# First layer of a graph network: a round's gathers in four groups, each issued at its own place of the round

## The chip, the cores and the metric

One core of a Trainium2 chip runs the whole program. The metric is the device time of one execution in microseconds (us). The core's engines are named as in the profile: PE (TensorE, matmuls; PEld its weight loads), DVE (VectorE), ACT (ScalarE), POOL (GpSimd), SP (SyncE, which here issues plain transfers). All transfers run on the core's 16 DMA engines.

## What is computed

3125 nodes with 256 features, 50000 edges sorted by their target node. Two layers, each followed by a residual and a layer norm:

```python
k, q, v = (typed_linear(x, W, ntype) for W in (Wk, Wq, Wv))       # (n, 8, 32)
# per edge e: source src[e], target dst[e], type r = etype[e] of 5
a  = ((k[src] @ Ratt[r]) * q[dst]).sum(-1) * pri[r] / sqrt(32)
w  = softmax of a over the edges that share a target
h  = segment_sum((v[src] @ Rmsg[r]) * w, dst)
h  = typed_linear(h, Wa, ntype)
x1 = layernorm(x + h * alpha + x * (1 - alpha))                   # alpha = sigmoid(skip)[ntype]

msg = (x1 @ weight[rel])[src] * norm * sigmoid(x1 @ gate_weight[rel])[src]   # 16 relations
out = layernorm(x1 + relu(segment_sum(msg, dst)))
```

## The kernel before

The nodes are cut into 26 tiles of 121 (ROUNDS = 26), and the edges of one tile, at most 2048 of them, are laid out as 128 partitions x 16 columns (U = 16, in G = 4 groups of GU = 4 columns). Three stages follow one another:

1. Tables. For each node and each of 5 edge types k·Ratt and v·Rmsg go to a table in HBM (`kv_table`, 2 KB a row), the queries to another.
2. First layer, 26 rounds, one per tile. For each of 16 columns POOL issues one indirect DMA (a gather): 128 rows of 2 KB, 256 KB in all, picked from `kv_table` into `kv[:, par, u]`, where par is the round's parity (two buffers). A line of 16 row numbers tells which rows. DVE multiplies with the queries that PE hands out (`score`, L1369 to L1376), takes a softmax along and across partitions, weighs the values (`weigh`, L1462), and PE sums them by target node (`aggregate`, L863) into the PSUM tile `b_agg`. The tile of the round before is finished meanwhile: `normalise` (L1382 to L1394, DVE) divides by the softmax sum, `turn_h` (L803) and `project` (L811, PE) apply Wa into `b_out`, `stats` (L1401, DVE) adds the residual, `norm_rows` gives x1. The tile two rounds back has its 16 relation products made: `message` (L835, PE, 8 chunks), `keep_message` (L1097, ACT) and `store_messages` (L495, SP, 4 stores of 484 KB into `message_table`).
3. Second layer, 26 turns: gathers from `message_table`, a sum by target, a norm.

Each engine works its own instructions off in the order in which the code gives them, and semaphores tie the engines together. PE's order in a round r (function `l0` of the PE block; f is the round before, n the next): turn_h(f, 0), message 0, hand_queries(r, 3), turn_h(f, 1), turn_ends(r) (L842), message 1, project(f), turn_carry(r) (L848), messages 2 and 3, turn_back(r) (L854), one-hot turns and queries of n, messages 4 and 5 between them, aggregate(r, 0 to 3) with queries of n between, messages 6 and 7. DVE's order: score(r, 0), score(r, 1), normalise(f), row_index(n), score(r, 2), score(r, 3), softmax scans, stats(f), make_onehot(n), softmax_across, norm_rows(f), softmax_less, weigh.

POOL's gathers are in `gather(pair)`: for each parity it waits for `idx_ready[par]` and then issues all 16 gathers of that round one behind another. `idx_ready` comes from DVE's `row_index` (L1358), which copies the 16 row numbers of the next round from `rows` into a small tile `idx`. That copy stands behind `normalise(f)`, which waits for `agg_done`, one count a round, given by the last aggregate matmul; it is therefore also what tells POOL that the buffer of round r + 1 (last used by round r - 1 = f) is free:

```python
dve.wait_ge(agg_done, f.done)          # in normalise(f), then behind it:
v.tensor_copy(idx[:, r.par, :], rows[:, 0, ...]).then_inc(idx_ready[r.par], 1)
```

The DMAs that SP issues in a round are: queries of the next round (242 KB), its x (121 KB), four message stores (4 x 484 KB), one x1 store (121 KB).

## Time and profile before

| | |
|---|---|
| median of 3 runs | 2108.01 us (2104.2 to 2119.34) |
| the profiled execution | 2111.33 us, its span 2109.7 us |
| PE busy | 1386.6 us, 66% |
| DVE busy | 926.7 us, 44% |
| POOL busy | 854.6 us, 41% |
| tables, until about | 340 us |
| first layer, about | 340 to 1462 us |
| second layer, about | 1462 to 2109.7 us |

The profile of one execution has a page (busy time of the engines, forty slices of the span, groups of instructions with their idle time and what ended it) and a trace that can be asked for the instructions of a stretch in order of time. Behind an instruction stands, in brackets, how long its engine sat idle before it and what ended that: a line of the kernel, "issue" (nothing that the profile shows), or "remote" (a semaphore moved, but no recorded instruction ended just then). PE's instructions are recorded when they start; their ends are modelled.

### The profile page before, as it was taken

The page shows a single profiled execution, that of the slowest core. Times are in us where ns is not written, and L with a number is a line of the kernel's source. Part 1 is how long each engine was busy: PE and PEld are TensorE (multiplying, and loading weights), DVE is VectorE, ACT ScalarE, POOL GpSimd, SP SyncE. Part 2 cuts the span into 40 slices and gives each one's busy share as a digit, 9 for nine tenths or more (in the row PEclk, how much of TensorE's full clock was granted, in tenths as well). Part 3 has the DMA queues.
Part 4 walks back from the last instruction along what each step waited for, and adds up shares of the span by engine and source line. Part 5 has one row for each costly group of instructions (what it writes and reads, how often), then busy time and mean ns, then how long its engine had stood idle before and what let it go on. Part 6 is the DMA issues. An engine that isn't in the chain of part 4 may idle for free.

```text
span 2109.7 us, 21535 instructions
## 1 busy us (share of the span) xinstructions
PE 1386.6 (66%) x6758; PEld 1135.8 (54%) x6758; DVE 926.7 (44%) x1940; ACT 494.7 (23%) x1069; POOL 854.6 (41%) x905
## 2 busy tenths in 40 slices
PE   4899985785797667777677776679425444445444
PEld 3888884574675556665466655567313322233323
DVE  5533454764564455454465544654212322223321
ACT  2223322232333333233243332335100000000000
POOL 1130004754244332233432334320575666666662
PEclk8999996798798878889888887789656666656666
DMA  5444465655445544445544455443433333333331
GB/s 122 124 147 144 135 227 157 183 181 174 136 142 176 161 146 137 133 134 160 178 145 142 149 157 176 141 136 95 115 109 89 104 104 104 104 94 107 108 104 53
DMA packets 103847, 286.54 MB, mean 136 GB/s; under 512 B 20804, under 2 KB 40408, under 8 KB 100660
## 3 DMA queue, kind: packets, MB, share of 16 engines
q0 software_dynamic: 56032, 169.34, 26.6%
q1 hardware_dynamic: 47774, 116.71, 18.3%
q8 instruction: 19, 0.31, 0.1%
q14 instruction: 22, 0.18, 0.0%
HBM read 189.33 MB, written 96.65 MB: 136 GB/s over the span
## 4 chain that ended last, share of the span: by engine, by line
PE 46%; issue 23%; another core or an unknown queue 12%; DVE 8%; DMA 5%; ACT 2%; POOL 2%; SPq 1%; DVEq 0%; ACTq 0%; POOLq 0%
PE bank L953 12%; PE bank L863 9%; PE bank L835 8%; PE bank L727 4%; PE bank L793 4%; DMA kv_table<-tstage 4%; PE bank L781 3%; DVE kv L1371 2%; PE bank L749 1%; POOL kv L649 1%; PE bank L735 1%; DVE onehot_r L1363 1%; PE bank L755 1%; DVE S L1376 1%
## 5 line engine op out<-in xcount | busy, mean ns | idle before, releaser
L633 POOL DMA_INDIRECT kv<-kv_table,idx x416 | 424.1, 1019 | 637.9 <-DVE idx L1358 514.7
L649 POOL DMA_INDIRECT kv<-message_table,rows x416 | 394.4, 948 | 274.1 <-issue 123.4
L953 PE MATMUL bank<-kv,onehot_w 128*121 128x256 f32 x832 | 274.7, 463 | 338.0 <-issue 307.2
L953 PEld LDWEIGHTS bank<-kv,onehot_w 128*121 128x121 f32 x832 | 186.2, 226 | 426.5 <-issue 391.0
L835 PE MATMUL bank<-wr_r,x1T_r 128*121 128x512 f32 x1248 | 359.5, 433 | 34.9 <-issue 22.7
L835 PEld LDWEIGHTS bank<-wr_r,x1T_r 128*121 128x121 f32 x1248 | 235.7, 200 | 95.2 <-issue 28.5
L1097 ACT ACTIVATE mstage<-bank,gate 121x256 f32<-121x256 f32 x416 | 171.4, 471 | 245.3 <-PE bank L835 132.7
L863 PE MATMUL bank<-kv,onehot_r 128*121 128x264 f32 x832 | 204.0, 394 | 0.0
L1512 DVE SCALAR_TENSOR_TENSOR z<-bank,xb 121x256 f32<-121x256 f32 x26 | 10.9, 420 | 425.5 <-remote 280.8
L863 PEld LDWEIGHTS bank<-kv,onehot_r 128*121 128x121 f32 x832 | 151.3, 187 | 29.5
L854 PE MATMUL bank<-ident,carry 8*128 8x8 f32 x26 | 6.2, 237 | 241.9 <-DVE carry L1441 220.3
L1371 DVE TENSOR_TENSOR kv<-kv,bank 128x512 f32<-128x512 f32 x208 | 132.1, 674 | 42.9 <-issue 33.4
L1175 ACT ACTIVATE sd<-mv,eps 121x1 f32<-121x1 f32 x26 | 7.7, 295 | 604.5 <-DVE mv L1518 506.2
L793 PE MATMUL bank<-qb_r,onehotT_r 121*128 121x256 f32 x832 | 139.5, 316 | 10.5 <-DVE kv L1371 10.5
L854 PEld LDWEIGHTS bank<-ident,carry 8*128 8x128 f32 x26 | 4.5, 172 | 253.7 <-issue 253.7
L1401 DVE TENSOR_TENSOR z<-z,bank 121x256 f32<-121x256 f32 x26 | 11.0, 421 | 293.4 <-remote 261.3
L793 PEld LDWEIGHTS bank<-qb_r,onehotT_r 121*128 121x128 f32 x832 | 125.1, 216 | 15.5 <-issue 11.5
L1376 DVE TENSOR_REDUCE S<-kv 128x32 f32<-128x1024 f32 x104 | 127.1, 1222 | 10.7
L1532 DVE TENSOR_SCALAR onehot_w<-iota_n,dstl,norms 128x121 f32<-128x121 f32 x416 | 111.9, 361 | 33.0 <-issue 21.6
L1462 DVE TENSOR_TENSOR kv<-kv 128x1024 f32<-128x1024 f32 x104 | 120.4, 1220 | 13.5 <-ACT kv L1107 12.0
L727 PE MATMUL bank<-xmT_r,w_r 128*128 128x484 f32 (+1 forms) x504 | 112.2, 386 | 12.7 <-DVE tstage L1298 10.6
L1055 ACT ACTIVATE onehotT_r<-bank 121x512 fp32r<-121x512 f32 x104 | 62.2, 598 | 222.9 <-PE bank L781 221.3
(136 smaller groups left out, 1647.1 us busy)
## 6 DMA issues: line engine op xcount, KB each, us to landing
message_table<-mstage SPq DMA_DIRECT2D x104, 484.0 KB
kv_table<-tstage SPq DMA_DIRECT2D x26, 1210.0 KB
kv<-kv_table,idx POOLq DMA_INDIRECT x416
kv<-message_table,rows POOLq DMA_INDIRECT x416
query_table<-qstage_r SPq DMA_DIRECT2D x26, 242.0 KB
qb_r<-query_table SPq DMA_DIRECT2D x26, 242.0 KB
kv<-in_Wr POOLq DMA_DIRECT2D x2, 2048.0 KB, 14.8
xb<-in_x SPq DMA_DIRECT2D x26, 121.0 KB
```

The source lines that it names most:

```text
L633: pool.indirect_dma_start(kv[:, par, u, 0:2 * C], None, ktab, bass.IndirectOffsetOnAxis(ap=idx[:, par, u:u + 1], axis=0)).then_inc(kv_land ...
L649: pool.indirect_dma_start(mrows[:, r.q, u, :], None, mtab, bass.IndirectOffsetOnAxis(ap=rows[:, 1, r.number, u:u + 1], axis=0)).then_inc(l ...
L727: last = mm(b[:, 0:plan.width], lhsT, rhs, start=(n == 0), stop=(n == len(terms) - 1))
L793: last = mm(b_qe[pr % 2][:, q * C:(q + 1) * C], onehotT_r[:, 2 * pr + q, :], qb_r[:, r.par, part, :], start=(part == 0), stop=(part == 1))
L835: last = mm(b_m[c % 2][:NODES, :], x1T_r[:, f.par, a, h, :], wr_r[:, w, h, 2 * c:2 * c + 2, :], start=(n == 0), stop=(n == len(terms) - 1))
L863: last = mm(b_agg[:NODES, 0:C + H], onehot_r[:, r.par, u, :].bitcast(F32), kv[:, r.par, u, C:ROW], start=(u == 0), stop=(u == U - 1))
L953: last = mm(b_l[r.q][:NODES, 0:C], onehot_w[:, r.q, u, :], mrows[:, r.q, u, :], start=(u == 0), stop=(u == U - 1))
L1097: last = a(mstage[:, b % 2, q % (RT // PARTS), :], b_m[c % 2][:NODES, k * C:(k + 1) * C], ACT.Copy, scale=gate[:NODES, f.par, q:q + 1])
L1371: ins = v.tensor_tensor(k, k, b_qe[pr % 2][:, :].rearrange("p (a c) -> p a c", a=2), ALU.mult)
L1376: v.tensor_reduce(S[:, :, u:u + 4].rearrange("p h u -> p u h"), kv[:, r.par, u:u + 4, 0:C].rearrange("p u (h d) -> p u h d", h=H), AX.X, A ...
L1462: v.tensor_tensor(w, w, e, ALU.mult).then_inc(weighted[g], 1)
L1532: last = v.tensor_scalar(onehot_w[:, r.q, u, :], iota_n[:, :], dstl[:, j, u], norms[:, j, u], ALU.is_equal, ALU.mult)
```

## The change

A round's 16 gathers are issued as four groups of four, and each group waits at its own place of the round. With n the round that is gathered for, into the buffer last used by round n - 2:

- group 0 waits until aggregate group 0 of round n - 2 is done,
- group 1 until all of round n - 2 is aggregated,
- group 2 also until `ends_turned` has counted n, so until turn_ends of round n - 1 (L842 of before) is done on PE,
- group 3 until `carryT` has counted n, so until turn_carry of round n - 1 (L848 of before) is done on PE.

For this `agg_done` counts each group of aggregate matmuls (4 a round). The gathers read their row numbers in `rows` itself, so `row_index`, its tile's use here and `idx_ready` go. POOL's loop over pairs of rounds is written out as 26 rounds.

```diff
-            def gather(pair):
-
-                for par in range(2):
-                    settle(pool, const_ready)
-                    if isinstance(pair, int) and par == 1:
-                        pool.wait_ge(wr_low, HALVES)
-                    pool.wait_ge(idx_ready[par], pair)
-                    for u in range(U):
-                        pool.indirect_dma_start(kv[:, par, u, 0:2 * C], None, ktab,
-                                                bass.IndirectOffsetOnAxis(ap=idx[:, par, u:u + 1], axis=0)
-                                                ).then_inc(kv_landed[par][u // GU], 16)
-
-            gather(1)
-            with pool.Fori(2, ROUNDS // 2 + 1) as pair:
-                gather(pair)
+            def gather_tables(n):
+
+                if n == 1:
+                    pool.wait_ge(wr_low, HALVES)
+                for g in range(G):
+                    if n >= 2:
+                        pool.wait_ge(agg_done, (n - 2) * G + (g + 1 if g == 0 else G))
+                        if g == 2:
+                            pool.wait_ge(ends_turned, n)
+                        if g == 3:
+                            pool.wait_ge(carryT, n)
+                    for u in range(g * GU, g * GU + GU):
+                        pool.indirect_dma_start(kv[:, n % 2, u, 0:2 * C], None, ktab,
+                                                bass.IndirectOffsetOnAxis(ap=rows[:, 0, n, u:u + 1], axis=0)
+                                                ).then_inc(kv_landed[n % 2][g], 16)
+            for n in range(ROUNDS):
+                gather_tables(n)
...
-            pool.wait_ge(agg_done, ROUNDS)
+            pool.wait_ge(agg_done, ROUNDS * G)
...
-                if g == G - 1:
-                    last.then_inc(agg_done, 1)
+                last.then_inc(agg_done, 1)
...
-            def row_index(r):
-
-                v.tensor_copy(idx[:, r.par, :], rows[:, 0, bass.ds(r.number, 1), :].rearrange("p j u -> p (j u)")
-                              ).then_inc(idx_ready[r.par], 1)
-
...
-                    dve.wait_ge(agg_done, f.done)
+                    dve.wait_ge(agg_done, f.nth(G, G))
...
                 if f:
                     normalise(f)
-                    if not r.final:
-                        row_index(r.next())
```

On POOL, before, the rounds' gathers stand like this in the loop over pairs (`idx_ready0` and `idx_ready1` are the semaphores of the two parities):

```order
L638 UNCONDITIONAL_BRANCH
L633 DMA kv<-kv_table,idx 128x512 [waits idx_ready0,const_ready]
L633 DMA kv<-kv_table,idx 128x512 x15
L633 DMA kv<-kv_table,idx 128x512 [waits idx_ready1,const_ready]
L633 DMA kv<-kv_table,idx 128x512 x15
L638 REGISTER_ALU
L638 COMPARE_AND_BRANCH
```

And now, where a later round's gathers stand; the first row is group 0 of one round, and `x3` are the other three of a group:

```order
L637 DMA kv<-kv_table,rows 128x512 [waits agg_done]
L637 DMA kv<-kv_table,rows 128x512 x3
L637 DMA kv<-kv_table,rows 128x512 [waits agg_done]
L637 DMA kv<-kv_table,rows 128x512 x3
L637 DMA kv<-kv_table,rows 128x512 [waits ends_turned,agg_done]
L637 DMA kv<-kv_table,rows 128x512 x3
L637 DMA kv<-kv_table,rows 128x512 [waits carryT,agg_done]
L637 DMA kv<-kv_table,rows 128x512 x3
```

One wait ahead of sixteen gathers has become a wait ahead of each four, and the waits are now on PE's work instead of DVE's copy.

On DVE, before, from `normalise` to the next scores in a round:

```order
L1384 TENSOR_SCALAR den<-bank 121x8
L1386 RECIPROCAL rden<-den 121x8
L1388 TENSOR_TENSOR z<-bank,rden 121x256
L1394 TENSOR_SCALAR hm<-z,calpha 121x256 x3
L1358 COPY idx<-rows 128x16
L1371 TENSOR_TENSOR kv<-kv,bank 128x2x256 x2
L1376 TENSOR_REDUCE S<-kv 128x4x8
L1371 TENSOR_TENSOR kv<-kv,bank 128x2x256 x2
```

And now:

```order
L1380 TENSOR_SCALAR den<-bank 121x8
L1382 RECIPROCAL rden<-den 121x8
L1384 TENSOR_TENSOR z<-bank,rden 121x256
L1390 TENSOR_SCALAR hm<-z,calpha 121x256 x3
L1367 TENSOR_TENSOR kv<-kv,bank 128x2x256 x2
L1372 TENSOR_REDUCE S<-kv 128x4x8
L1367 TENSOR_TENSOR kv<-kv,bank 128x2x256 x2
```

The copy into `idx` is gone; all else stands in the same order. PE, ACT and SP have the same instructions in the same order as before.

## Rows read from the trace of the kernel before

**Rows 1.** Stretches: us, PE, PEld, DVE, ACT, POOL busy (instructions), PEclk, DMA share, GB/s.

```profile
458.40:1425.70 967.30, 694.83 (x3522) 577.71 (x3522) 513.07 (x880) 324.13 (x726) 345.68 (x352) 0.85 0.49 152
...
1462.00:2109.70 647.70, 294.24 (x917) 200.39 (x915) 154.45 (x554) 22.91 (x59) 394.43 (x416) 0.65 0.35 100
```

**Rows 2.** Source L1384 (first instruction of normalise), 458 to 1430 us: count, ns, first, last.

```profile
L1384 DVE TENSOR_SCALAR den<-bank x23: 166/167/167, 458.4 to 1425.7; 121x8 f32<-121x8 f32 x23
```

**Rows 3.** Groups by line, 458 to 1426 us: count | busy us, mean ns | idle before <-releasers.

```profile
L633 POOL DMA_INDIRECT kv<-kv_table,idx x352 | 345.7, 982 | 609.5 <-DVE idx L1358 506.2 <-issue 103.3
...
L1401 DVE TENSOR_TENSOR z<-z,bank 121x256 f32<-121x256 f32 x22 | 9.3, 421 | 278.6 <-remote 256.4 <-issue 22.1
...
L1358 DVE COPY idx<-rows 128x16 int32 (+1 forms) x22 | 3.7, 168 | 0.0
```

**Rows 4.** Timeline of a typical round: start us, length, engine, line, what, [idle before <-releaser].

```profile
806.71 0.17 DVE L1384 TENSOR_SCALAR den<-bank 121x8 f32<-121x8 f32 x1 [0.94 <-PE bank L863]
...
809.46 0.94 POOL L633 DMA_INDIRECT kv<-kv_table,idx  x1 [27.06 <-DVE idx L1358]
...
811.42 0.30 SPq L495 DMA_DIRECT2D message_table<-mstage  x1
...
813.33 1.64 PE L835 MATMUL bank<-wr_r,x1T_r 128*121 128x512 f32 x6
...
814.82 2.75 PE L811 MATMUL bank<-wa,hmT 128*121 128x256 f32 x12
...
818.76 0.84 ACT L1097 ACTIVATE mstage<-bank,gate 121x256 f32<-121x256 f32 x2 [3.21 <-remote]
...
819.76 22.94 SPq L495 DMA_DIRECT2D message_table<-mstage  x3
...
828.38 0.94 POOL L633 DMA_INDIRECT kv<-kv_table,idx  x1 [0.30 <-issue]
829.40 0.42 DVE L1401 TENSOR_TENSOR z<-z,bank 121x256 f32<-121x256 f32 x1 [13.33 <-remote]
...
841.20 3.72 PE L863 MATMUL bank<-kv,onehot_r 128*121 128x264 f32 x16
...
850.97 0.17 DVE L1384 TENSOR_SCALAR den<-bank 121x8 f32<-121x8 f32 x1 [0.94 <-PE bank L863]
```

**Rows 5.** Stretches: typical round, short round, and the gathers of each.

```profile
806.70:851.00 44.30, 31.67 (x162) 26.50 (x161) 23.35 (x41) 14.83 (x33) 15.30 (x16) 0.85 0.48 151
1079.60:1114.20 34.60, 30.51 (x162) 25.24 (x162) 23.22 (x40) 14.81 (x33) 18.65 (x16) 0.95 0.62 193
809.50:829.40 19.90, 11.31 (x58) 8.69 (x56) 4.84 (x7) 6.19 (x15) 15.26 (x16) 0.91 0.82 262
1082.40:1107.00 24.60, 20.51 (x102) 16.42 (x101) 16.09 (x26) 13.00 (x30) 18.63 (x16) 0.93 0.75 233
```

**Rows 6.** Timeline of an early round, without message stores.

```profile
399.10 0.94 POOL L633 DMA_INDIRECT kv<-kv_table,idx  x1 [3.91 <-DVE idx L1358]
...
401.27 2.82 PE L811 MATMUL bank<-wa,hmT 128*121 128x256 f32 x12 [0.43 <-ACT hmT L1060]
...
404.13 0.42 DVE L1401 TENSOR_TENSOR z<-z,bank 121x256 f32<-121x256 f32 x1
```

**Rows 7.** Timeline of a short round.

```profile
1079.62 0.17 DVE L1384 TENSOR_SCALAR den<-bank 121x8 f32<-121x8 f32 x1 [0.94 <-PE bank L863]
...
1082.38 0.94 POOL L633 DMA_INDIRECT kv<-kv_table,idx  x1 [27.39 <-DVE idx L1358]
...
1085.01 0.94 POOL L633 DMA_INDIRECT kv<-kv_table,idx  x1 [1.69 <-issue]
...
1087.73 2.75 PE L811 MATMUL bank<-wa,hmT 128*121 128x256 f32 x12
...
1093.52 0.42 DVE L1401 TENSOR_TENSOR z<-z,bank 121x256 f32<-121x256 f32 x1 [4.53 <-remote]
...
1114.21 0.17 DVE L1384 TENSOR_SCALAR den<-bank 121x8 f32<-121x8 f32 x1 [0.94 <-PE bank L863]
```

More of the change, by code:

```diff
@@ L315, in build @@
         q_loaded, x_loaded = sems("q_loaded", 2), sems("x_loaded", 2)
-        idx_ready, oh_ready = sems("idx_ready", 2), sem("oh_ready")
+        oh_ready = sem("oh_ready")
         kv_landed = [sems(f"kv_landed{p}_", G) for p in range(2)]
@@ L1487, in l0 @@
                     keep_x1T_low(f)
-            row_index(Round(dve, 0, 0))
-            row_index(Round(dve, 0, 1))
             make_onehot(Round(dve, 0, 0))
```

## Prediction

> **What bounds the kernel now.** I read the stretches first. The second layer, 647.7 us, holds its own gathers and nothing that the change touches [rows 1]. The first layer is the place: the first instruction of `normalise` runs once a round, and its 23 starts from 458.4 to 1425.7 us are 22 rounds of 43.97 us [rows 2]. In those 967.3 us PE is busy 694.8 us, 31.6 us a round, DVE 23.3, POOL 15.7 [rows 1]. So no engine is full, and PE is the nearest.
>
> Where the other 12 us of PE are, the groups by line tell. DVE stands idle 278.6 us ahead of the 22 additions of L1401 (`stats`), 12.66 us a round, and 256.4 us of it are put down to "remote"; POOL's idle time (609.5 us) is the wait for the copy L1358 and costs nothing by itself [rows 3]. L1401 waits for `project` on PE. In the typical round `project` starts at 814.82 and is modelled to end 2.75 us later, at 817.57; L1401 starts at 829.40, after 13.33 us idle [rows 4]. The reader is to see that the semaphore comes 11.8 us after the modelled end. It is not project alone: message 1 (L835 at 813.33), ahead of project in PE's order, is kept by ACT only at 818.76, after 3.21 us of "remote" idle [rows 4]. PE finishes late in this stretch, and nowhere does the profile name who holds it.
>
> What is special about the stretch are the gathers. They are issued from 809.46 to 829.32, without a pause, and in these 19.9 us the DMA engines move 262 GB/s at a share of 0.82 (the whole round: 151 GB/s) [rows 4, 5]. SP puts a message store beside them at 811.42 and another at 819.76 [rows 4]. L1401 starts within 0.1 us of the last gather's end. Two other rounds are the control. Early, with gathers from 399.10 but no message stores yet, project ends at 401.27 + 2.82 = 404.09 and L1401 starts at 404.13: not late [rows 6]. And a short round, where POOL's second gather came 1.69 us late: project ends at 1090.48, L1401 at 1093.52, only 3.0 us late (idle 4.53), the gathers take 24.6 us, at 233 GB/s, and the whole round 34.6 us instead of 44.3 [rows 7, 5]. I read this as: PE's completions are late when an unbroken row of gathers meets SP's transfers, the lateness builds up over the row, and it ends when the row ends. Why, the trace doesn't show.
>
> **The change, part by part.**
>
> *The copy into `idx` goes.* DVE loses 0.168 us a round [rows 3], at most 22 x 0.168 = 3.7 us. I take nothing: DVE idles 12.66 us a round for PE, which covers it, and with that idle time down to 4.5 us it still does.
>
> *Gathers read `rows` itself.* The same 16 gathers, at 0.94 us and a pause of 0.30 each [rows 4], 20 us a round on POOL, which has 44. No cost.
>
> *`agg_done` four times a round.* A count on an instruction that already stands there: nothing.
>
> *Group 0* now starts behind aggregate group 0. Groups 0 and 1 are the 3.72 us from 841.20, so it starts near 843.1, where before the first gather came 2.75 us behind `normalise` (809.46 against 806.71), that is at 853.7 for this buffer. It is 4 x 1.25 = 5.0 us of gathers in a stretch of PE work that had none, together with the fourth message store. It ends before the aggregation does (850.97). Bounds of what it costs: nothing, as in the early round, and at most what message 1 shows after a row of equal length: it is modelled to end at 813.33 + 1.64 = 814.97, 5.5 us after the first gather, and came 818.76 - 814.97 = 3.8 us late [rows 4]. Nearer is the short round, where five gathers in the first 5 us brought 3.0 us; but project there had four SP transfers beside it, group 0 has one. I take 1 us.
>
> *Group 1* starts at the end of the aggregation, 850.9, and runs 5.0 us under messages 6 and 7, `turn_h` and message 0. SP's store comes 4.7 us behind `normalise` (811.42 against 806.71 [rows 4]), so this group is nearly alone, as in the early round: I take nothing, bound 3.8 us.
>
> *Group 2* starts behind turn_ends, just ahead of message 1 and project, with the store, the x1 store and the loads beside it: this is where the lateness was. But only four gathers can be in front of project, and POOL then waits for turn_carry, which stands behind project on PE. Queued behind POOL's waiting instruction are only its own gathers, and their data are needed in the next round: `score(n, 2)` stands behind the next `normalise`. So the row breaks where before it went on for another 12 us. The group is 5.0 us long; project lasts 2.75. If PE is released when the group ends plus what the group still has in flight, project comes 5.0 - 2.75, about 2.3 to 5 us late. The short round's 3.0 us [rows 7] lies in it, and I take that.
>
> *Group 3* starts behind turn_carry, under messages 2 and 3, stats and the one-hots, when PE has slack: it waits there for DVE's carry in any case. Taken from the short round, where the gathers also went on through this stretch.
>
> **The sum.** The short round holds all of this but group 0: L1401's idle 4.53 us in place of 13.33, gathers through 24.6 of 34.6 us, PE's clock at 0.95 in place of 0.85, PE busy 30.5 us of it [rows 5]. So a round after the change is 34.6 + 1 (group 0) = 35.6 us, and 22 of them give 22 x (43.97 - 35.6) = 184 us. The rounds before 458 us and the last one stay. Profiled execution: 2111.3 - 184 = 1927 us; the median lies 3 us under the profiled execution, so **1924 us**.
>
> Ends: if the whole idle time at L1401 goes, a round takes 43.97 - 12.66 = 31.3 us (PE's 30.5 us stand just below), 279 us less: 1829 us. If group 0 and 1 each cost the 3.8 us of message 1 and project is 5 us late, a round is 34.6 + 2 x 3.8 + 2 = 44.2 us: no gain.
>
> **The rivals.**
>
> *A: more than that.* The pauses clear the lateness fully, as in the early round, and PE, never idle for long, keeps its clock (0.85 on average over the layer, 0.95 in the short round [rows 1, 5]). Rounds of 31.3 to 33.6 us: 1829 to 1880 us. For it: project is on time with gathers alone [rows 6]. Against it: no later round is on time; the shortest had 3.0 us. 0.17.
>
> *B: half of it.* Groups 0 and 1 spread the lateness to PE's full stretch, where each late semaphore is on the way to `normalise` and `turn_h`: rounds of 37.5 to 43.5 us, 1966 to 2098 us. For it: DMA traffic a round is the same and PE has no slack there. 0.15.
>
> *C: gathers are not the cause.* Project is late for another reason, which the change leaves alone: SP's stores or the message matmuls themselves, of which the early round had none [rows 6]. The gathers then move and nothing else does: 43.97 us a round stay, about 2108 us. Against it: the short round had all stores and messages, and only its gathers ran otherwise [rows 7]. 0.07, with a further 0.02 for a gain or loss of B's kind within 1%. The Trainium skill, "SBUF — State Buffer", section "Who interferes with whom", says that PE and ACT never wait on anyone and that a DMA never contends with a compute engine; by that this rival would be the forecast and the time 2108 us. The typical round against the early one [rows 4, 6] doesn't bear it out: with gathers and stores PE's results come 11.8 us late, with gathers alone not at all.
>
> *D: slower.* The lateness is a price for each row, not for its length: every one of the four groups puts PE back by the 3.8 us of message 1, all on PE's chain. 4 x 3.8 = 15.2 us against the 12.66 us that go; a round is 46.5 us and the time 2108 + 22 x 2.5 = 2164 us. It decides from 12.66 / 4 = 3.2 us a group on. Against it: the two groups that come before SP's transfers look like the early round. 0.05.
>
> **How the numbers follow.** The forecast has 0.54 (rounds of 33.6 to 37.5 us: 1880 to 1966 us), A 0.17, B 0.15, C 0.09, D 0.05. The range reaches from 1850, which leaves out the lower half of A, to 2020, which leaves out the upper third of B, C and D: about 0.2 outside. About 1% is what a measurement of this kernel can tell from no change. Faster by over 1% (under 2087 us): 0.54 + 0.17 + 0.14 = 0.85; within 1%: 0.10; slower: 0.05.
>
> **What would show it.** In the profile after: the idle time ahead of the addition in `stats` falls from 278.6 us to about 100 us for 22 rounds; the gathers stand in fours, with pauses, the first near 8 us ahead of `normalise`; 22 rounds take 780 us and not 967; the granted clock of the first layer rises from 0.85 to about 0.95; the second layer stays at 648 us. Wrong would be: 12 us ahead of `stats` as before (C), or the idle time gone there and come back ahead of `normalise`, `turn_h` or the queries' scores (B, D).

## The result, and the profile after

The changed kernel takes 1803.35 us (median of 4 runs, 1799.8 to 1804.13), beside 2107.84 us for the kernel before (2104.2 to 2119.34): a ratio of 0.855, 95% interval 0.852 to 0.8575. The gain is 304.5 us; 184 had been forecast, and the time lies below the range. The profiled execution has a span of 1798.2 us (before: 2109.7). One execution of small_stores_before (2137.8 us) and one of second_sixteens_again (2208.4 us, at a granted clock of 0.61) ran over 1.5% slower than the fastest of their kernel and are left out of the ratios below.

From the page of the profile after: busy times, then in forty slices of 45 us TensorE's granted clock, in tenths.

```profile
PE 1322.6 (74%) x6758; PEld 1088.5 (61%) x6758; DVE 921.7 (51%) x1914; ACT 492.7 (27%) x1069; POOL 890.4 (50%) x905
...
PEclk9899999769999999999999999965556666666666
```

The rows that answer to [rows 2] and [rows 1] (first instruction of `normalise`, now L1380; stretches of the first layer and of one round: us, PE, PEld, DVE, ACT, POOL busy, clock, DMA share, GB/s):

```profile
L1380 DVE TENSOR_SCALAR den<-bank x24: 166/167/167, 427.7 to 1112.6; 121x8 f32<-121x8 f32 x24
```

```profile
448.00:1110.00 662.00, 637.43 (x3556) 537.18 (x3554) 513.10 (x867) 322.76 (x728) 381.58 (x352) 1.00 0.72 223
724.60:754.40 29.80, 28.69 (x162) 24.16 (x161) 23.08 (x39) 14.71 (x33) 17.26 (x16) 1.00 0.72 225
```

23 rounds in 684.9 us are 29.78 us a round, where it was 43.97. PE is busy 637 of 662 us, at the full granted clock: it is the bound now. The groups by line from 448 to 1110 us, which answer to [rows 3] (the gathers are L637, the addition in `stats` L1397):

```profile
L637 POOL DMA_INDIRECT kv<-kv_table,rows x352 | 381.6, 1084 | 274.9 <-PE bank L865 125.3 <-issue 89.2 <-PE bank L844 59.5
...
L1397 DVE TENSOR_TENSOR z<-z,bank 121x256 f32<-121x256 f32 x22 | 9.3, 422 | 32.7 <-issue 17.9 <-PE bank L813 14.8
```

DVE waits 32.7 / 22 = 1.49 us ahead of `stats`, not 12.66, and what it waits for is project's recorded end. One round in order of time, beside [rows 4]:

```profile
724.58 0.17 DVE L1380 TENSOR_SCALAR den<-bank 121x8 f32<-121x8 f32 x1 [0.94 <-PE bank L865]
724.81 0.95 POOL L637 DMA_INDIRECT kv<-kv_table,rows  x1 [3.08 <-PE bank L865]
...
728.59 0.94 POOL L637 DMA_INDIRECT kv<-kv_table,rows  x1 [0.30 <-issue]
...
732.25 0.95 POOL L637 DMA_INDIRECT kv<-kv_table,rows  x1 [2.72 <-PE bank L844]
...
732.71 2.75 PE L813 MATMUL bank<-wa,hmT 128*121 128x256 f32 x12
...
733.93 12.22 SPq L495 DMA_DIRECT2D message_table<-mstage  x3
...
735.50 0.42 DVE L1397 TENSOR_TENSOR z<-z,bank 121x256 f32<-121x256 f32 x1 [1.46 <-PE bank L813]
...
737.29 2.33 POOL L637 DMA_INDIRECT kv<-kv_table,rows  x1 [0.30 <-issue]
...
746.86 0.95 POOL L637 DMA_INDIRECT kv<-kv_table,rows  x1 [2.81 <-PE bank L865]
```

Group 1 runs from 724.81, group 2 from 732.25 behind turn_ends (L844), group 3 right behind it, group 0 of the next round from 746.86, behind the first aggregate group. Project (L813) ends at 732.71 + 2.75 = 735.46, and `stats` starts at 735.50: not late, though three of group 2's gathers and two of SP's transfers were issued beside it, and the fourth (736.04) is still to come.

**Where the 14.2 us of a round went.** 12.66 - 1.49 = 11.2 us are idle time ahead of `stats`. PE's busy time went from 694.8 / 22 = 31.6 us a round [rows 1, 2] to 637.43 / 662 x 29.78 = 28.7, which is 2.9 us, for the same matmuls at a granted clock of 1.00 in place of 0.85. Together 14.1. (Counted on PE alone it is the same: idle 12.4 us a round before, 1.1 now, and 2.9 us less of work.) The second layer is as before, from 1149 us to the end, 649 us.

### The profile page after: what moved, and what is told of

The parts are those of the page before. It is cut to its first block, busy times and chain, and to the rows that moved or that the text cites. A ratio compares the mean times of both kernels' runs of the same rounds, so it can differ in the third digit from the quotient of the medians.

```text
span 1798.2 us, 21483 instructions
## 1 busy us (share of the span) xinstructions
PE 1322.6 (74%) x6758; PEld 1088.5 (61%) x6758; DVE 921.7 (51%) x1914; ACT 492.7 (27%) x1069; POOL 890.4 (50%) x905
## 4 chain that ended last, share of the span: by engine, by line
PE 56%; issue 24%; DVE 7%; DMA 6%; POOL 3%; ACT 1%; SPq 1%; another core or an unknown queue 1%; DVEq 0%; ACTq 0%; POOLq 0%
PE bank L954 14%; PE bank L837 11%; PE bank L865 10%; PE bank L795 5%; PE bank L729 5%; DMA kv_table<-tstage 4%; PE bank L783 2%; POOL kv L651 2%; PE bank L813 2%; PE bank L751 2%; PE bank L737 1%; DVE kv L1367 1%; PE bank L757 1%; POOL kv L637 1%; DVE S L1372 1%
## 5 line engine op out<-in xcount | busy, mean ns | idle before, releaser
L637 POOL DMA_INDIRECT kv<-kv_table,rows x416 | 458.6, 1102 | 304.9 <-PE bank L865 130.9
L837 PE MATMUL bank<-wr_r,x1T_r 128*121 128x512 f32 x1248 | 324.8, 403 | 2.2 <-ACT mstage L1098 2.2
L837 PEld LDWEIGHTS bank<-wr_r,x1T_r 128*121 128x121 f32 x1248 | 217.7, 183 | 51.9 <-ACT mstage L1098 3.3
L1504 DVE SCALAR_TENSOR_TENSOR z<-bank,xb 121x256 f32<-121x256 f32 x26 | 10.9, 420 | 429.7 <-remote 280.1
L795 PE MATMUL bank<-qb_r,onehotT_r 121*128 121x256 f32 x832 | 130.3, 301 | 14.6 <-DVE kv L1367 11.8
L795 PEld LDWEIGHTS bank<-qb_r,onehotT_r 121*128 121x128 f32 x832 | 115.3, 199 | 19.8 <-issue 14.1
L1524 DVE TENSOR_SCALAR onehot_w<-iota_n,dstl,norms 128x121 f32<-128x121 f32 x416 | 111.1, 361 | 29.9 <-issue 18.5
L729 PE MATMUL bank<-xmT_r,w_r 128*128 128x484 f32 (+1 forms) x504 | 108.3, 377 | 10.5 <-DVE tstage L1299 8.4
L729 PEld LDWEIGHTS bank<-xmT_r,w_r 128*128 128x128 f32 x504 | 91.8, 195 | 25.9 <-DVE tstage L1299 7.2
L751 PE MATMUL bank<-rel_r,kvT_r 128*121 128x384 f32 x312 | 65.1, 352 | 25.8 <-DVE kvT_r L1239 25.8
L783 PE MATMUL bank<-ident_r,onehot_r 128*121 128x128 f32 x416 | 71.3, 296 | 16.6 <-DVE onehot_r L1359 10.8
```

The lines of the kernel that those rows point to most:

```text
L637: pool.indirect_dma_start(kv[:, n % 2, u, 0:2 * C], None, ktab, bass.IndirectOffsetOnAxis(ap=rows[:, 0, n, u:u + 1], axis=0)).then_inc(kv_ ...
L729: last = mm(b[:, 0:plan.width], lhsT, rhs, start=(n == 0), stop=(n == len(terms) - 1))
L795: last = mm(b_qe[pr % 2][:, q * C:(q + 1) * C], onehotT_r[:, 2 * pr + q, :], qb_r[:, r.par, part, :], start=(part == 0), stop=(part == 1))
L837: last = mm(b_m[c % 2][:NODES, :], x1T_r[:, f.par, a, h, :], wr_r[:, w, h, 2 * c:2 * c + 2, :], start=(n == 0), stop=(n == len(terms) - 1))
L1524: last = v.tensor_scalar(onehot_w[:, r.q, u, :], iota_n[:, :], dstl[:, j, u], norms[:, j, u], ALU.is_equal, ALU.mult)
```

## The experiments

Eighteen runs in five groups, each group on one chip. The kernel before took 2172.9, 2106.0, 2165.2 and 2116.1 us on four of the chips, and 1715.1 us on the fifth (below). In every diff, but for small_stores_before, `-` is the changed kernel. "A round" is worked out as above, from the first and last start of `normalise` in the first layer: over 21 rounds for the four kernels near 44 us, over 23 for the others. These 23 reach to the last start and so hold the last, shorter round (25.7 us in most kernels), which the 23 of the changed kernel above do not: it lowers the mean by 0.2 us in kernels near 30 us a round, by up to 0.5 in those near 36.

### Which of the waits matters

The changed kernel's waits ahead of group g were replaced:

```diff
                     if n >= 2:
-                        pool.wait_ge(agg_done, (n - 2) * G + (g + 1 if g == 0 else G))
-                        if g == 2:
-                            pool.wait_ge(ends_turned, n)
-                        if g == 3:
-                            pool.wait_ge(carryT, n)
+                        pool.wait_ge(agg_done, (n - 2) * G + G)          # one_row: no more than this
```

> The changed kernel, but a round's 16 gathers wait once, for all of round n - 2 to be aggregated, and go out in one row; row numbers are still read where they stand, the copy on VectorE is gone and the loop is written out. Theory R (the unbroken row of gathers beside SyncE's transfers makes TensorE's results late until the row ends): rounds of about 43 to 44 us as before, 11 to 13 us idle ahead of the addition in stats, 2080 to 2110 us. Rival S (what helps is that the gathers no longer wait for VectorE's copy and start earlier, or the smaller changes beside it): rounds near 30 us, about 1805 us.

Measured: 2117.4 us, ratio 0.975 (0.970 to 0.980), 43.8 us a round. So the row numbers read in place, the loop written out and `agg_done` by groups don't bring the gain; but 55 us are gained, and 22 rounds in which the row starts and so ends 2.5 us sooner (0.2 us behind `normalise` in place of 2.75 [rows 4]) would give just that. That is arithmetic: no trace of the kernel before was kept from this chip.

For g01_together only the first line changes (group 0 waits for all of the aggregation), for g23_together only the wait on `carryT` goes.

> The changed kernel, but group 0 no longer goes out during the aggregation: groups 0 and 1 go out together behind all of round n - 2, groups 2 and 3 wait as in the change. Group 2 is then free to go as soon as group 1 is issued, so 12 gathers stand in one row across project. Theory R: that row ends some 15 us after normalise and project comes about 4 to 7 us late, rounds of 34 to 37 us, 1890 to 1960 us. Rival P (only the last group, held back until project is done, counts): rounds near 30 us, about 1810 us.

> The changed kernel, but group 3 no longer waits for turn_carry: groups 2 and 3 are a row of eight from turn_ends on, across project. Theory R: project comes late by what is left of the row, up to 7 us, rounds of 33 to 37 us, 1870 to 1960 us. Rival P: the same, as group 3 is what it says matters. Rival Q (pauses anywhere are enough, and eight in a row are still short): rounds near 30 us, about 1805 us.

g01_together: 1947.9 us, ratio 0.897 (0.894 to 0.900), 35.8 us a round. g23_together: 1799.8 us, ratio 0.829 (0.825 to 0.832), 29.7 us. The changed kernel's wait for `carryT` can go; group 0's early start can't go by itself, as that leaves eight gathers in a row. The timeline of a round of g01_together:

```profile
719.18 0.17 DVE L1380 TENSOR_SCALAR den<-bank 121x8 f32<-121x8 f32 x1 [0.94 <-PE bank L865]
719.41 0.95 POOL L637 DMA_INDIRECT kv<-kv_table,rows  x1 [13.01 <-PE bank L865]
...
728.19 0.94 POOL L637 DMA_INDIRECT kv<-kv_table,rows  x1 [0.31 <-issue]
...
731.61 4.46 PE L813 MATMUL bank<-wa,hmT 128*121 128x256 f32 x12 [4.14 <-ACT hmT L1061]
```

Project starts 12.4 us behind `normalise`, where in the changed kernel it is 8.1 (732.71 - 724.58), and takes 4.46 us, not 2.75. In one_row, with sixteen in a row, it starts 13 to 22 us behind in all but the first two and the last two rounds. Project itself waits, by the code, for ACT's copy of what turn_h made (`hmT`), and ACT waits for turn_h's result: a late result of PE comes back to PE as a late start.

Each group behind the landing of the one before:

```diff
+                        pool.wait_ge(agg_done, (n - 2) * G + G)
+                        if g:
+                            pool.wait_ge(kv_landed[n % 2][g - 1], 16 * GU * (n // 2 + 1))
```

> The changed kernel with all four groups at the place of before (behind all of round n - 2), but each group waits until the group ahead of it has landed. No wait on TensorE's work. Theory R in the form 'gathers pile up in the DMA queues': with at most four gathers under way at a time TensorE's results are on time, rounds of 30 to 32 us, 1800 to 1850 us. Rival P (it is the place, away from project, that counts): project is still covered by gathers and comes late, rounds of 38 us or more, over 1980 us.

Measured: 1949.4 us, ratio 0.898 (0.892 to 0.903), 36.5 us a round. POOL waits some 6 us for each landing, falls behind, and the last group of a round meets the first of the next: again eight in a row, again 36 us. It says no more than g01_together.

Three more placings, with the waits ahead of a group:

```diff
+ hole_only:  g0: agg_done (all);  g1, g2, g3: also ends_turned            # one hole, then twelve
+ no_hole:    g0: as changed;  g1, g2: agg_done (all);  g3: also carryT    # no wait on turn_ends
+ late_row:   all groups: agg_done (all), carryT                           # sixteen behind turn_carry
```

> The changed kernel, but group 0 waits for all of round n - 2 (as before), and groups 1, 2 and 3 then wait together for turn_ends of round n - 1 and go out as one row of twelve. What is left of the change is one pause, from about 5.3 to 7.7 us behind normalise, while SyncE sends a message store, the x1 store and the queries' load. Theory H (the late stretch sets in when gathers are still being issued while SyncE's transfers at 4.7 to 6.5 us start; a pause there is enough, whatever the length of the row behind it): rounds near 30 us, 1800 to 1830 us. Theory R (long rows beside stores are the cause): the row of twelve covers project and brings 36 us or more, over 1930 us.

> The changed kernel, but group 2 no longer waits for turn_ends: group 0 goes out during the aggregation, groups 1 and 2 are one row of eight from 0.2 us behind normalise on, and group 3 waits for turn_carry. Project has no more gathers beside it than in the changed kernel, but there is no pause at 5.3 to 7.7 us. Theory H: late results from 5 us on, rounds of 34 to 37 us, 1890 to 1960 us. Theory R or P (row length, or only what lies beside project): near 30 us, about 1805 us.

> The changed kernel, but all 16 gathers of a round wait for turn_carry of round n - 1 and go out in one row of 20 us, behind project and under the later message stores. Theory H: the row starts behind SyncE's group of transfers and is nearly over when the next one starts; rounds of 30 to 33 us, 1800 to 1870 us. Theory R (an unbroken row beside message stores): TensorE late in that row, over 2000 us.

hole_only: 1795.8 us, ratio 0.853 (0.848 to 0.859), 29.7 us a round, all of the gain. Twelve gathers follow one another without a wait, but not at full pace: while DVE makes one-hots and weighs, single gathers last up to 2.3 us (737.29 above), and the twelve start 1.53 us apart on average (7.6 to 24.5 us behind `normalise`). no_hole: 1954.1 us, 0.929 (0.923 to 0.934), 35.8 us, with eight in a row. late_row: 1917.5 us, 0.911 (0.906 to 0.917), 34.7 us; project is on time. The semaphores of PE's results come late only from 28 us behind `normalise` on, 1.1 us and then up to 5.4, some four gathers into the last full-pace row (from 732.16) and where SP issues nothing:

```profile
718.24 2.75 PE L810 MATMUL bank<-wa,hmT 128*121 128x256 f32 x12
719.47 12.21 SPq L495 DMA_DIRECT2D message_table<-mstage  x3
721.03 0.42 DVE L1394 TENSOR_TENSOR z<-z,bank 121x256 f32<-121x256 f32 x1 [2.29 <-PE bank L810]
...
732.16 0.95 POOL L634 DMA_INDIRECT kv<-kv_table,rows  x1 [0.30 <-issue]
...
740.93 0.95 POOL L634 DMA_INDIRECT kv<-kv_table,rows  x1 [0.30 <-issue]
742.06 0.17 DVE L1377 TENSOR_SCALAR den<-bank 121x8 f32<-121x8 f32 x1
```

So it is not project's place, nor SP's transfers, but gathers in a row at the pace of 1.25 us. The early round [rows 6] does not speak against that: its project ended at 404.09, when only four gathers had been issued.

### Bytes and stores

small_stores_before is the kernel before with each message store cut from 484 KB to 30 KB (the second layer then reads its rows from `kv_table`); what it leaves out is most of the message table.

```diff
-  sp.dma_start(mtab_n[..., b * w:(b + 1) * w], mstage[:, b % 2, :, :]...)
+  sp.dma_start(mtab_n[..., b * w:b * w + C // 4], mstage[:, b % 2, 0, 0:C // 4])
```

> The kernel before, but each message store writes only 256 bytes a node in place of 4 KB (30 KB in place of 484 KB), and the second layer gathers from the first layer's table so that its work stays alike. The rest of the messages isn't stored, so the output is not the reference's. If the bytes of the message stores beside the gathers make TensorE late: project on time as in the earliest rounds, rounds of 30 to 32 us, 1790 to 1850 us. If it is the x1 store, the queries' load or the mere issue of transfers on SyncE, or the gathers alone: rounds of about 44 us, near the kernel before.

2110.1 us, ratio 1.000 (0.998 to 1.003), 44.6 us a round: the stores' bytes do nothing. half_bytes is one_row with gathers of half a row from the third round on; it leaves out the values, which stay those of older rounds:

```diff
-  pool.indirect_dma_start(kv[:, n % 2, u, 0:2 * C], None, ktab, ...)
+  width, table = (2 * C, ktab) if n < 2 else (C, ktab.rearrange("n (k c) -> (n k) c", k=2))
+  pool.indirect_dma_start(kv[:, n % 2, u, 0:width], None, table, ...)
```

> Sixteen gathers in one unbroken row behind the end of the aggregation; from the third round on each fetches 1 KB a row and not 2 KB (the values stay those of older rounds, so the output isn't the reference's). The number of gathers and their pace stay, the bytes are halved. If bytes or the DMA engines' load are what makes PE's results late: project on time, rounds of 30 to 32 us, about 1800 to 1850 us. If the number of transfers or POOL's issuing is: rounds of 43 to 44 us, about 2100 us. Something between, if both.

2121.2 us, ratio 0.979 (0.976 to 0.983), 43.9 us a round, as with 2 KB rows (one_row 43.8), while the share of the DMA engines over these rounds is 0.36, in one_row 0.51. The stretches of one round, from the sixth gather on:

```profile
781.00:784.00 3.00, 2.53 (x17) 1.84 (x15) 0.00 (x0) 0.84 (x2) 2.35 (x3) 1.00 0.74 220
784.00:786.00 2.00, 0.00 (x0) 0.00 (x0) 0.52 (x1) 0.00 (x0) 1.43 (x2) 1.00 0.82 220
786.00:792.00 6.00, 0.00 (x0) 0.00 (x0) 2.81 (x5) 0.16 (x1) 4.47 (x6) 0.55 0.49 154
```

And what stands around that gap, in its timeline:

```profile
781.45 0.47 PE L802 MATMUL bank<-ident,hm 121*128 121x121 f32 x3
...
791.84 0.47 ACT L1058 ACTIVATE hmT<-bank 128x363 f32<-128x363 f32 x1 [9.11 <-issue]
...
792.46 4.99 PE L810 MATMUL bank<-wa,hmT 128*121 128x256 f32 x12 [8.93 <-issue]
```

The profile puts both waits down to "issue", but the code names them: turn_h (L802) is modelled to end at 781.92, ACT's copy of it starts only at 791.84, 9.9 us later, and project waits for that copy and starts 0.15 us behind it. So PE is not kept from starting here; its result comes late, and it then waits for itself by way of ACT. The share of the DMA engines falls to 0.49 meanwhile, and the result is late all the same. PE's granted clock, 0.55 from 786 to 792 us, is by then near the lower of its two levels (0.5, 1.2 GHz), and project takes 4.99 us where it takes 2.75 at 1.00. That is the second half of the cost: a PE that has stood idle is slower afterwards.

One more suspect can be settled by the trace of the kernel before: that PE waits for its instructions to be fetched. From 510 to 1380 us, some twenty late rounds, that trace has packets of two DMA queues only, the gathers' (25396) and SP's (18266), and none of the two instruction queues, which do show elsewhere in it (41 packets in all).

### The place in the round, the hole and the pace

In these kernels POOL waits for none of PE's work between groups; it clears a small scratch tile (128x128, 0.21 us each; six of them put the next gather off by 1.55 us):

```diff
+  pool.wait_ge(agg_done, (n - 2) * G + G)
+  if g:                                   # paused_shifted: ahead of g0 too
+      for again in range(6):              # paused_short: 2, paused_mid: 4
+          pool.memset(rest[:, :], 0.0).then_inc(rested, 1)
+          pool.wait_ge(rested, ...)       # its own last one
+  # spread: two of them ahead of every single gather, no other pause
```

> All four groups wait, as in the row of sixteen, for the end of the aggregation alone; but from the third round on POOL clears a 512-byte-a-partition scratch tile six times ahead of groups 1, 2 and 3 (0.25 us each by the profile's row of a 128x128 clearing, so 1.5 us or more), and waits for none of PE's work. Theory K (an unbroken row of five or more gathers makes PE's results late, a hole ends it): rounds of about 30 us, the idle time ahead of the addition in stats under 2 us, time near 1800 us. Rival T (what matters is that groups 2 and 3 stand behind turn_ends and turn_carry on PE, so that none is issued beside project): groups 0 to 2 go out in the first 18 us, across project, so rounds of 36 to 44 us, 1950 to 2100 us.

> As the paused one, with a pause also ahead of group 0: the gathers of group 0 then lie from about 2 to 7 us behind normalise, with hand_queries, turn_ends and SP's store beside them. Theory K: still rounds of about 30 us and a time near 1800 to 1830 us, since no row is longer than four. Rival H (what matters is that no gather is issued from 5.3 to 7.7 us behind normalise): project late again by 3 us or more, rounds of 35 us or more, 1930 us or more.

> As the paused one, but only two clearings (0.5 us and what the semaphore takes) ahead of groups 1, 2 and 3. If any hole ends a row, rounds of about 30 us, 1800 us. If the hole has to let what is in flight drain (at 256 KB a gather and 224 GB/s a gather takes 1.2 us of all DMA engines, and two to three are in flight), 0.6 us is too short: rounds near those of the unbroken row, 36 to 44 us, 1950 to 2110 us.

paused_0: 1792.4 us, ratio 0.828 (0.824 to 0.831), 29.7 us a round. paused_shifted: 1796.5 us, 0.829 (0.826 to 0.833), 29.9 us. So no wait on PE is needed, and the place of the gathers in the round doesn't matter (rival H of the expectations falls). paused_short: 2117.2 us, 0.978 (0.973 to 0.982), 44.4 us, no better than one_row:

```profile
770.03 0.17 DVE L1385 TENSOR_SCALAR den<-bank 121x8 f32<-121x8 f32 x1 [0.94 <-PE bank L870]
770.27 0.95 POOL L642 DMA_INDIRECT kv<-kv_table,rows  x1 [23.31 <-PE bank L870]
...
774.98 0.49 POOL L639 MEMSET rest<- 128x128 f32 x2
775.74 0.95 POOL L642 DMA_INDIRECT kv<-kv_table,rows  x1 [0.27 <-issue]
...
782.45 5.45 PE L818 MATMUL bank<-wa,hmT 128*121 128x256 f32 x12 [4.16 <-issue]
...
793.41 0.42 DVE L1402 TENSOR_TENSOR z<-z,bank 121x256 f32<-121x256 f32 x1 [10.13 <-remote]
```

Four gathers take 775.74 - 770.27 = 5.47 us there, 1.37 us each. Is it the hole that has to be longer, or the mean pace that has to be slower? spread gives every gather the short pause: no hole, one gather each 1.70 us.

> All sixteen gathers behind the end of the aggregation, with two clearings of the scratch tile (0.45 us more from start to start, as ahead of the groups in the short-paused kernel) ahead of every single gather: one gather each 1.70 us, where groups of four with six clearings had the same mean, four in 6.6 us. If the mean pace decides (POOL's gathers come faster than something drains, and a backlog grows): project on time, rounds of 30 to 31 us, about 1800 to 1830 us. If only a hole of 1.5 us or more ends a row: rounds of 36 to 45 us, 1950 us or more.

> As the paused kernels, with four clearings (about 1.0 us more from start to start) ahead of groups 1, 2 and 3; two clearings (0.45 us) had been too few, six (1.55 us) enough. If the pace decides, 16 gathers in 16 x 1.25 + 3 x 1.0 us are nearer the paused one: 30 to 36 us a round, 1800 to 1930 us. If there is a threshold of the hole above 1 us: 43 us a round, about 2100 us.

Neither could be told on the chip of that group, since the kernel before took only 1715.1 us on it (1711.9 to 1719.7, 10 runs). spread: 1728.2 us, 1.008 (1.006 to 1.010), paused_mid 1716.0 us, 1.001 (0.999 to 1.002). So the same code was run again:

> The same code as the spread kernel (two clearings ahead of every gather, one gather each 1.70 us), since on the chip of that call the kernel before took 1715 us and had nothing to cure. If the kernel before takes 2100 us or more here: the mean pace decides if rounds are 30 to 31 us (about 1800 to 1830 us); a hole of 1.5 us does if they are 36 to 45 us (1950 us or more). If the kernel before takes near 1715 us here too, about 1728 us, and nothing is told.

1804.1 us beside 2116.1, ratio 0.852 (0.845 to 0.860), 30.2 us a round:

```profile
665.79 0.17 DVE L1388 TENSOR_SCALAR den<-bank 121x8 f32<-121x8 f32 x1 [0.94 <-PE bank L873]
...
667.01 0.98 POOL L645 DMA_INDIRECT kv<-kv_table,rows  x1 [0.27 <-POOL rest L632]
667.99 0.48 POOL L632 MEMSET rest<- 128x128 f32 x2
668.74 0.95 POOL L645 DMA_INDIRECT kv<-kv_table,rows  x1 [0.27 <-POOL rest L632]
...
673.93 2.75 PE L821 MATMUL bank<-wa,hmT 128*121 128x256 f32 x12
...
676.72 0.42 DVE L1405 TENSOR_TENSOR z<-z,bank 121x256 f32<-121x256 f32 x1 [1.51 <-PE bank L821]
```

Project ends at 676.68 and `stats` starts at 676.72, with gathers at an even pace from one `normalise` to the next. Two of the rounds took 36.9 and 34.7 us and not 29.8; in the one that starts at 569 us it is not PE: DVE waits 8.89 us for a gather to land. At 1.70 us there is little room left. It is the pace, not the hole: at 1.25 and 1.37 us a gather PE's results are late from about the fifth on, at 6.6 / 4 = 1.65 (paused_0) and 1.70 they are not, nor in hole_only with twelve at 1.53. Where between 1.37 and 1.53 the change lies stays open.

### The second layer, and a chip that has none of it

In the second layer POOL gathers at 1.25 us too. The changed kernel's timeline there, PE alone (the kernel before has the same: 307.2 us of idle time put to "issue" in its group L953):

```profile
1402.50 15.65 PE L954 MATMUL bank<-kv,onehot_w 128*121 128x256 f32 x56 [0.82 <-issue]
...
1428.95 0.28 PEld L954 LDWEIGHTS bank<-kv,onehot_w 128*121 128x121 f32 x1 [1.82 <-issue]
...
1430.35 0.58 PE L954 MATMUL bank<-kv,onehot_w 128*121 128x256 f32 x1 [2.21 <-issue]
...
1431.75 0.28 PEld L954 LDWEIGHTS bank<-kv,onehot_w 128*121 128x121 f32 x1 [2.52 <-issue]
```

PE starts one instruction, a weight load or a matmul, each 1.40 us (sometimes after 0.70), from about 1418 to 1448 us, some 3 us beyond the row's last gather, and the idle time between them is put to "issue", not to a transfer; by the code these instructions wait for nothing but the one ahead. So here PE is in fact kept from starting. Ahead of it, between two rows and up to the eleventh gather of the next (which starts at 1404.94), it did 56 matmuls in 15.65 us: in this layer the row runs for ten gathers before it tells, not four. (The expectations say a matmul each 1.4 us; it is an instruction.) DVE is not spared. Its one-hots have no wait between them either, and 18.5 us of idle time put to "issue" stand ahead of them in the changed kernel, 21.6 in the kernel before; in paused_mid, on the chip of 1715 us, it is 0.7. From their pages of the profile:

```profile
L1524 DVE TENSOR_SCALAR onehot_w<-iota_n,dstl,norms 128x121 f32<-128x121 f32 x416 | 111.1, 361 | 29.9 <-issue 18.5
```

```profile
L1532 DVE TENSOR_SCALAR onehot_w<-iota_n,dstl,norms 128x121 f32<-128x121 f32 x416 | 108.8, 366 | 12.0 <-PE bank L845 11.4
```

PE's groups in the second layer, first of the changed kernel, then of paused_mid, whose second layer is the same code, on the chip of 1715 us:

```profile
L954 PE MATMUL bank<-kv,onehot_w 128*121 128x256 f32 x832 | 276.1, 463 | 336.7 <-issue 300.8 <-DMA kv<-message_table,rows 33.7
```

```profile
L962 PE MATMUL bank<-kv,onehot_w 128*121 128x256 f32 x832 | 302.1, 541 | 234.7 <-DMA kv<-message_table,rows 234.7
```

And the latter's timeline:

```profile
1399.25 6.55 PE L962 MATMUL bank<-kv,onehot_w 128*121 128x256 f32 x16 [3.59 <-DMA kv<-message_table,rows]
1409.28 6.67 PE L962 MATMUL bank<-kv,onehot_w 128*121 128x256 f32 x16 [3.48 <-DMA kv<-message_table,rows]
```

There PE works beside the same rows of gathers without a gap, 16 matmuls in 6.6 us, and all its idle time has a transfer behind it. The hold is a matter of the chip: the first measurement and four of the five groups have it, and the chip of one group has none in the second layer. That it has none in the first either is read from the times: paused_mid has rounds of 29.8 us there (without the last one), and the kernel before, of which no trace was kept from this chip, is just as fast. The changed kernel itself wasn't run on it.

Two kernels add pauses of six clearings to the second layer of the changed kernel:

```diff
                 for u in range(U):
+                    if u % 8 == 0:                  # second_sixteens: u % 16
+                        pause(6)
                     pool.indirect_dma_start(mrows[:, r.q, u, :], None, mtab,
```

> The changed kernel, and in the second layer six clearings ahead of the first and the ninth gather of each turn. There POOL issues rows of 32 without a pause, and PE, which waits for nothing that the profile shows, starts a matmul only each 1.4 us while a row runs (0.25 us when it has ended). If rows of gathers hold back PE whatever stage it is in: PE's matmuls run at full pace for the first four gathers of each eight and the idle time put to issue falls from 300 us to under 150; POOL then sets the turn, 16 x 1.25 + 2 x 1.55 = 23.1 us against 22.7 now, so the time hardly moves: 1800 to 1815 us. If PE's crawl in the second layer has another cause (its data, its clock): issue idle as before, and the pauses add 26 x 3.1 = 80 us or nothing.

> As the one with eights, but one pause a turn: rows of sixteen. POOL's turn is 16 x 1.25 + 1.55 = 21.6 us against 22.7 now, if PE's sixteen pairs of matmuls (about 7.5 us at full pace) fit into the first four or five gathers and the pause, with nine more at 1.4 us: 26 x 1.1 = 29 us less at best, 1775 us; if PE is still late at the end of each row, no gain: 1800 us or 1810.

> The same code as the second-layer kernel with one pause a turn. If the kernel before takes 2100 us or more here and rows of gathers hold back PE in the second layer too: 1760 to 1775 us, where the changed kernel has about 1800, and less than the 300 us of idle time put to issue ahead of PE's matmuls. If the second layer's crawl has another cause: 1800 to 1810 us. If the kernel before takes near 1715 us here: 1758 us.

On the chip without the hold they show what POOL's pauses cost: 1795.6 us, ratio 1.046 (1.042 to 1.049), and 1758.1 us, 1.024 (1.020 to 1.028). second_sixteens_again took 1810.6 us, in a single execution without a trace, beside 2116.1 for the kernel before: no gain over the changed kernel, as far as one execution tells. By the pace that fits: (16 x 1.25 + 1.55) / 16 = 1.35 us a gather, still too fast. And a pace of 1.65 would make a turn of 26.4 us, where two turns now take 45.4 us (L1504 at 1404.81 and at 1450.20), 22.7 each: slower than being held. So by this estimate the layer has nothing to gain in this way. The fastest runs, paused_0 with 1792.4 and hole_only with 1795.8 us, lie 0.4 to 0.6% under the changed kernel, measured on other chips; no chip ran both.

## Why the prediction was wrong

- **The place and the bound**: right. First layer, PE's late results at `stats`, second layer unchanged (647.7 and 649 us).
- **"PE's completions are late when an unbroken row of gathers meets SP's transfers"**: half right. The row does it; late_row has it where SP issues nothing, small_stores_before with hardly any bytes in the stores, and in spread_again the same transfers meet gathers all through the round and PE's results are on time. The early round [rows 6], taken as the control for the stores, was none: only four gathers had gone out when its project ended. "It ends when the row ends" held. What the row needs is a pace faster than somewhere between 1.37 and 1.53 us a gather.
- **The copy goes, no cost or gain**: its DVE time, yes. That the row starts 2.5 us sooner was left out; alone one_row brought 2.5%, which fits it. In the changed kernel nothing is left of it, as the lateness goes altogether.
- **Group 0 costs 1 us**: it costs nothing. paused_0, with group 0 behind the aggregation, and the changed kernel both have 29.8 us a round, if the last is left out.
- **Group 2 leaves project 2.3 to 5 us late, 3.0 taken from the short round**: this is the first term that failed, and with it the mechanism behind it, that PE is released only when the group ends. A group of four delays nothing: `stats` starts at 735.50 with the group still running, and waits 1.49 us, not 4.53. The short round [rows 7] was the wrong template: its row ran on at 1.25 us after one wider gap, long enough for the hold to begin; it was a milder case of the trouble and not a picture of its absence. The early round [rows 6] was the better one, as no more than four gathers had run in it.
- **Groups 1 and 3 cost nothing**: right.
- **The lower end, 43.97 - 12.66 = 31.3 us, with "PE's 30.5 us just below"**: the second that failed. Both numbers hold a PE at a clock of 0.85 to 0.95, slow because it had been held. With the waits gone it is busy 28.7 us a round at 1.00. Rival A, with 0.17, named the mechanism ("the pauses clear the lateness fully", "keeps its clock") but priced only the idle time; with 2.9 us for the clock, and the 1.5 us that `stats` still waits, it would have been 43.97 - 11.17 - 2.9 = 29.9 us a round, and 29.8 came.
- **Sum**: it started from the short round of 34.6 us and kept two things of it that went: 3.0 us of lateness (4.53 - 1.49), and PE's work at a clock of 0.95, 30.5 us and now 28.7, so 1.8 us. It added 1 us for group 0 that wasn't there. 35.6 - 3.0 - 1.8 - 1 = 29.8 us, which is what was measured.
- **The chances**: the range was said to leave out about 0.2. By the prediction's own bounds it is near 0.3: the lower 0.4 of A (0.07), the upper 0.6 of B (0.09, not a third), C (0.09) and D (0.05).
- **Rival C** and the rule beside it: the Trainium skill, "SBUF — State Buffer", section "Who interferes with whom", says that PE and ACT never wait on anyone. On the chips with the hold the traces show otherwise in effect (project's result 11.8 us late in the typical round [rows 4], one instruction of PE each 1.40 us in the second layer), on one it agrees. That the hold goes by SBUF's ports, which that section is about, no run shows.
- **Rivals B and D**: no group, wherever it was put, cost anything at the slow pace.

**What stays open** is how POOL's issuing reaches PE. Excluded by a run: bytes and the load of the DMA engines (half_bytes), the bytes of the stores (small_stores_before), SP's transfers (late_row), a dependence on PE's own work (paused_0, spread_again), the place in the round (paused_shifted). Excluded by the trace of before for the first layer: the fetching of instructions. What is left is something that each gather of 128 rows takes for about 1.4 to 1.5 us whatever its bytes, that POOL at 1.25 us overruns, and that PE's instructions or their completions need too, and in the second layer DVE's. That is argued from the paces and not shown; it would fit the nearly equal 1.40 us a PE instruction. Gathers of fewer rows weren't tried. Whether the late results of the first layer and the late starts of the second are one thing, why the second layer's row runs for ten gathers first, and whether the recording of the profile takes part in either, no run tells.

## What to carry to other kernels

Idle time put to "issue" or "remote" is first to be held against the code: the wait may be there and only unnamed, as project's for ACT's copy was, and the chain then leads to whose result is late. Where it stands beside a full-pace row of indirect gathers, one experiment is worth while: slow the gathers (a wait, or a short piece of work of the issuing engine) to about the pace that the stage needs; here 16 gathers fit into a round of 29.8 us at 1.65 us each, so the slower pace cost nothing. Price a removed stall with the clock that the engine will have without it, from a stretch where it had it, and take as template the stretch in which the trouble is absent, not the one where it is mild. And time such a change on more than one chip: on one of those used here there was nothing to gain.

## What the runs showed of the hardware

- An engine that issues gathers can hold others back: in the first layer, from about the fifth gather at 1.25 us on, PE's results reach the waiting engine late, by 11.8 us in the typical round of before and 9.9 us in half_bytes; in the second, from about the eleventh on, PE starts one instruction each 1.40 us, and DVE's one-hots too start late. At a mean of 1.53 us or more a gather the first layer has none of it (hole_only, paused_0, spread_again).
- Halving the bytes of each gather changed nothing: 43.9 us a round against 43.8, on two chips.
- The hold differs by chip: the kernel before took 2106 to 2173 us on the chips of four groups and 1715 us on another.
- A PE kept waiting pays twice: after 8.9 us without work project takes 4.99 us and not 2.75, the granted clock near its lower level (0.55).
